# The two halves of a tile's attention scores joined in TensorE's order, in a fused two-layer kernel

## The chip, the cores and the metric

The kernel runs on one core of one Trainium2 chip, as one launch. The metric is device time in microseconds (us). Timed three times, the kernel before took 2907.69, 2910.03 and 2917.73 us; the median, 2910.03, is what a change is held against.

## The reference

The input x has 2048 rows of 128 numbers. Four blocks work on it, all in f32:

```
xn = layernorm(x);  x = x + attention0(xn) + experts0(xn)       # 16 heads, causal over 2048; 8 experts, top 2
xn = layernorm(x);  x = x + mamba(xn) + transformer(xn)

def transformer(x):                                             # 6 layers
    for i in range(6):
        x = attn_layer(shift_tokens(x), Wqkv[i], q_scale[i], k_scale[i], Wo[i]) + x
        x = ffn_layer(shift_tokens(x), ln_g[i], ln_b[i], W1[i], b1[i], W2[i], b2[i]) + x

def attn_layer(x, ...):                                         # 16 heads of 64
    q, k, v = split(x @ Wqkv)                                   # 128 -> 3 x 1024
    q, k = rotate(l2norm(q) * q_scale), rotate(l2norm(k) * k_scale)
    # windows of 32 rows: each query sees its own window and the one before it, masked to a band
    sim = einsum('bhwie,bhwje->bhwij', q, [k of the last window, k]) * 8
    return softmax(sim) @ [v of the last window, v] @ Wo
```

`ffn_layer` is a layer norm, a gated product of 128 to 2 x 341 and back to 128. The change touches only `sim`'s place in the order of work.

## The kernel before, in words

There are two stages, divided by a barrier of all engines. The first, up to about 1145 us, holds attention0, the experts and half of mamba. The second, `transformer_*`, holds the six layers with the other half of mamba woven in. The change lies in the second stage alone.

The second stage goes through 96 tiles (`NTILE`: 6 layers of 16 tiles of 128 rows) in a software pipeline. One turn of the loop `for n in range(LAST_STEP)` in `transformer_pe` is a step. The order on each engine is written out by hand: nothing is planned by costs, and no engine takes anything out of its order. Between engines there are semaphores (`E.wait_ge`, `.then_inc`). TensorE's order in step n is:

1. `scores_first(n)`: 8 bf16 matmuls write the mask into the score banks (L1372); then it waits for the turned queries and keys (semaphores `qT`, `kT`, `halo`) and `score_half` issues 32 small matmuls, of 64 rows by 32 columns, for the first eight heads (L1363). An f32 matmul stands in the profile as two MATMUL and two LDWEIGHTS records, so this half is 64 of each.
2. `project_q(n + 2)`: the queries of the tile after next, 128x128 by 128x512, four records of each kind (L1348).
3. `scores_second(n)`: the other 32 small matmuls (64 records), after which `lscore` tells VectorE that the scores are there.
4. `side(n)`: one transpose of a coming input (L1426), sometimes a product for mamba (L1434), and the output projection of the tile before (L1442, 16 records).
5. `project_k(n + 2)` (L1348), then `turn_probs(n)` (L1389), whose transposes wait for the exponentials.
6. `project("v", n + 1)` (L1348), `values(n, 0)` (L1400, 64 records), the feed-forward part (`forward`: L1456, L1457, L1463, L1448), `values(n, 1)` (L1400), the transposes of the next queries and keys (L1356), the transposes of the output (L1409).

VectorE's order in a step: mamba's scan of the unit (L476), `shift` (a maximum over the scores, L1833, and the subtraction in two halves, L1839), `finish` (the residual, L1880, behind L1442), `rotate("q", n + 2)` (L1852 to L1854, behind the queries' squares), the copies of the turned probabilities (L1873), and so on. ScalarE's order: `square("q", n + 2)` (L1630) first, behind the queries' projection; then mamba's two decays (L457), the turned input (L1638, behind L1426), and the exponentials (`probs`, L1673, behind `shift`). GpSimd adds and scales the rotated queries and keys (L2030, L2049). SyncE issues the DMAs.

PSUM is taken as four pairs of banks. `pair_table` gives each product its pair by the parity of n: the scores and `turn_probs` have one pair, the queries' projection another, `side` a third. `pair(key, *until)` waits until the last holder's contents have been read, and notes what has to be read before the pair is free again.

Of the kernel before, what the change touches and what calls it, by code (L numbers as in the profile page):

```python
# [34 lines left out]
DH = 64  # L35
INNER = H * DH
WIN = 32
# [4 lines left out]
NTILE = L * NT  # L42
# [1122 lines left out]
def halos(n):  # L1165

    return n - n // NT
# [161 lines left out]
def transformer_pe(k):  # L1329
    E, s, ps = k.te, k.sem, k.ps  # L1330
    held = {}

    def pair(key, *until):

        p = k.pair[key]
        for name, value in held.get(p, ()):
            E.wait_ge(s(name), value)
        held[p] = until
        return ps[:, 2 * p:2 * p + 2, :]

    def project(what, n, *until):
        l = n // NT
        at = ("q", "k", "v").index(what) * INNER
        to = pair((what, n), *until)
        E.wait_ge(s("xcT"), n + 1)
        E.wait_ge(s(f"wqkv{l % 2}"), 32 * (l // 2 + 1) if l else 16)
        for c in range(2):
            mm = E.matmul(to[:, c, :], k.xcT[:, n % 4, :], k.wqkv[l % 2][:, at + 512 * c:at + 512 * (c + 1)], start=True, stop=True)  # L1348
        mm.then_inc(s(what + "_mm"), 1)
# [6 lines left out]
            mm = E.transpose(to[:, j // 4, j % 4 * P:(j % 4 + 1) * P], k.ra[:, n % 2, w, j * P:(j + 1) * P], k.ident[:])  # L1356
        mm.then_inc(s(f"rows_{what}"), 1)

    def score_half(n, half, to):
        for j in range(4 * half, 4 * half + 4):  # L1360
            for w in range(4):
                for o in range(2):
                    mm = E.matmul(to[WIN * w:WIN * (w + 1), o, j * DH:(j + 1) * DH], k.qT[o * DH:(o + 1) * DH, j, WIN * w:WIN * (w + 1)],  # L1363
                                  k.kT[o * DH:(o + 1) * DH, n % 2, j, WIN * w:WIN * w + DH], start=False, stop=True, skip_group_check=True)
        return mm

    def scores_first(n):
        to = pair(("scores", n), ("shifted_s", 2 * n + 2))
        for w in range(4):
            for o in range(2):  # L1370
                here, of = slice(o * DH, (o + 1) * DH), o * DH + (WIN if w else 0)
                E.matmul(to[WIN * w:WIN * (w + 1), o, :], k.identb[here, of:of + WIN], k.band[here, 0 if n % NT == 0 else 1, :], start=True, stop=False,  # L1372
                         skip_group_check=True)
        E.wait_ge(s("qT"), n + 1)
        E.wait_ge(s("kT"), n + 1)
        if halos(n):
            E.wait_ge(s("halo"), halos(n))
        score_half(n, 0, to)

    def scores_second(n):  # L1380
        p = k.pair["scores", n]
        score_half(n, 1, ps[:, 2 * p:2 * p + 2, :]).then_inc(s("lscore"), 1)

    def turn_probs(n):
        to = pair(("turn_probs", n), ("prT", 2 * n + 2))
        for c in range(8):
            if c % 4 == 0:
                E.wait_ge(s("exp"), 2 * n + c // 4 + 1)
            mm = E.transpose(to[:, c // 4, c % 4 * P:(c % 4 + 1) * P], k.pr[:, c * P:(c + 1) * P], k.ident[:])  # L1389
            if c % 4 == 3:  # L1390
                mm.then_inc(s("prob_mm"), 1)

    def values(n, o):
        to = pair((f"values{o}", n), (f"on{o}", n + 1))
        E.wait_ge(s("prT"), 2 * n + o + 1)
        E.wait_ge(s(f"vw{n % 2}"), 160 * (n // 2 + 1))
        for c in range(4):
            for w in range(4):
                for i in range(2):
                    mm = E.matmul(to[WIN * w:WIN * (w + 1), i, c * (DH + 1):(c + 1) * (DH + 1)],  # L1400
                                  k.prT[i * DH:(i + 1) * DH, 4 * o + c, WIN * w:WIN * (w + 1)],
                                  k.vw[i * DH:(i + 1) * DH, n % 2, w, 4 * o + c, :], start=True, stop=True, skip_group_check=True)
        mm.then_inc(s(f"values{o}"), 1)

    def turn_out(n):
        to = pair(("turn_out", n), ("oT", n + 1))
        E.wait_ge(s("on1"), n + 1)
        for c in range(8):
            mm = E.transpose(to[:, c // 4, c % 4 * P:(c % 4 + 1) * P], k.on[:, c * P:(c + 1) * P], k.ident[:])  # L1409
        mm.then_inc(s("out_turned"), 1)  # L1410

    def side(n):

        until = []
        if n >= 1:
            until.append(("ys", n))
        if n + 3 < NTILE:
            until.append(("xcT", n + 4))
        if new_frame(n + 1) and n + 1 < NTILE:
            until.append(("halo", halos(n + 1)))  # L1420
        if n in CHUNK_OUT:
            until.append(("mo", CHUNK_OUT[n] - NCH // 2 + 1))
        to = pair(("side", n), *until)
        if n + 3 < NTILE:
            E.wait_ge(s(f"xc{(n + 3) % 2}"), 48 * ((n + 3) // 2 + 1))
            E.transpose(to[:, 1, 0:P], k.xc[:, (n + 3) % 2, :], k.ident[:]).then_inc(s("xc_turned"), 1)  # L1426
        if new_frame(n + 1) and n + 1 < NTILE:
            E.wait_ge(s("kT"), n + 1)
            E.matmul(to[:, 1, P:3 * P], k.turn[:], k.kT[:, n % 2, :, P:KW], start=True, stop=True, skip_group_check=True).then_inc(s("halo_mm"), 1)
        if n in CHUNK_OUT:  # L1430
            E.wait_ge(s("y_gated"), CHUNK_OUT[n] - NCH // 2 + 1)
            for t in range(2):
                for a in range(ET):
                    mm = E.matmul(to[:, 0, (1 + t) * P:(2 + t) * P], k.yg[:, a, t * P:(t + 1) * P], k.wout[:, a, :], start=a == 0, stop=a == ET - 1,  # L1434
                                  skip_group_check=True)
            mm.then_inc(s("mo_mm"), 1)
        if n >= 1:
            l = (n - 1) // NT
            E.wait_ge(s("oT"), n)
            E.wait_ge(s(f"wqkv{l % 2}"), 32 * (l // 2 + 1))  # L1440
            for c in range(8):
                mm = E.matmul(to[:, 0, 0:P], k.oT[:, c * P:(c + 1) * P], k.wo[:, l % 2, c, :], start=c == 0, stop=c == 7, skip_group_check=True)  # L1442
            mm.then_inc(s("fin_mm"), 1)
# [34 lines left out]
    def forward(n):  # L1478

        what, m = forward_step(n)  # L1480
        if n >= NTILE + 4:
            if what:
                j = int(what[2])
                up(m, j, pair(("extra", n), ("hv", 3 * m + j + 1)))
            down_last(n - NTILE - 4)
        elif n % 4 == 2:
            until = [("xfT", m + 1)] if what else []
            if m >= 1:
                until.append(("x_down", m))
            to = pair(("extra", n), *until) if until else None  # L1490
            if m >= 1:
                down(m - 1, to)
            if what:
                turn_normal(m, to)
        elif what:
            j = int(what[2])
            up(m, j, pair(("extra", n), ("hv", 3 * m + j + 1)))

    def project_q(n):
        project("q", n, ("rotated_q", n + 1))  # L1500

    def project_k(n):
        project("k", n, ("rotated_k", n + 1))
# [18 lines left out]
    def turn_hat():  # L1522
        to = pair(("extra", HAT_STEP), ("turned_out", TURNED + 4))
        E.wait_ge(s("hat"), 1)
        for q in range(2):
            for c in range(4):
                mm = E.transpose(to[:, q, c * P:(c + 1) * P], k.hat[:, 4 * q + c, :], k.ident[:])
            mm.then_inc(s("turned"), 1)
# [35 lines left out]
    turn_rows("k", 0)  # L1564
    for n in range(LAST_STEP):
        if n < NTILE:
            scores_first(n)
        if n + 2 < NTILE:
            project_q(n + 2)
        if n < NTILE:  # L1570
            scores_second(n)
        if n <= NTILE:
            side(n)
        if n + 2 < NTILE:
            project_k(n + 2)
        if n < NTILE:
            turn_probs(n)
        if n + 1 < NTILE:
            project("v", n + 1, ("v_out", n + 2))
        if n < NTILE:  # L1580
            values(n, 0)
        if n != NTILE - 1:
            forward(n)
        if n == HAT_STEP:
            turn_hat()
        if n in IN_EXTRA:
            project_in("extra", n, IN_EXTRA[n])
        if n < NTILE:
            values(n, 1)
        if n + 1 < NTILE:  # L1590
            turn_rows("q", n + 1)
            turn_rows("k", n + 1)
        if n in IN_LATE:
            E.wait_ge(s("small"), 80)
            project_in("late", n, IN_LATE[n])
        if n == FACTOR_STEP:
            factors(n)
        if n in RATE_STEPS:
            rates(n, RATE_STEPS[n])
        if n < NTILE:  # L1600
            turn_out(n)
        if n == NTILE - 1:
            forward(n)
# [742 lines left out]
```

## Time and profile before

| what | value |
|---|---|
| timed runs | 2907.69, 2910.03, 2917.73 us |
| profiled execution, first to last instruction (span) | 2911.7 us |
| TensorE busy | 2789.5 us, 96% |
| VectorE, ScalarE, GpSimd busy | 2336.3, 1746.4, 1680.3 us |
| mean granted TensorE clock | 0.996 of full |
| matmul records, weight-load records | 40886, 40886 |

The profiled execution is told by its span; of time outside it the profile shows nothing. The span is 1.7 us above the median of the timed runs. "Busy" is the time in which an engine had at least one instruction in work. The ends of matmuls are modelled, so the distance from one start to the next tells more than a duration does.

### The profile page before, as it was taken

The page shows a single profiled execution, that of the slowest core. Times are in us where ns is not written, and L with a number is a line of the kernel's source. Part 1 is how long each engine was busy: PE and PEld are TensorE (multiplying, and loading weights), DVE is VectorE, ACT ScalarE, POOL GpSimd, SP SyncE. Part 2 cuts the span into 40 slices and gives each one's busy share as a digit, 9 for nine tenths or more (in the row PEclk, how much of TensorE's full clock was granted, in tenths as well). Part 3 has the DMA queues.
Part 4 walks back from the last instruction along what each step waited for, and adds up shares of the span by engine and source line. Part 5 has one row for each costly group of instructions (what it writes and reads, how often), then busy time and mean ns, then how long its engine had stood idle before and what let it go on. Part 6 is the DMA issues. An engine that isn't in the chain of part 4 may idle for free.

```text
span 2911.7 us, 98296 instructions
## 1 busy us (share of the span) xinstructions
PE 2789.5 (96%) x40886; PEld 1832.5 (63%) x40886; DVE 2336.3 (80%) x3830; ACT 1746.4 (60%) x2618; POOL 1680.3 (58%) x1454
## 2 busy tenths in 40 slices
PE   8999999999999999899999999999999999999997
PEld 5556565655665655566656666666666666666665
DVE  6777755774677776998968999889998999898884
ACT  4455555555666665556666666666666666666663
POOL 1000002000466665676767888878887888788882
PEclk9999999999999999999999999999999999999999
DMA  3000000000011111243234434333443343333332
GB/s 97 1 1 1 1 1 3 1 1 10 21 45 46 45 46 31 77 129 79 73 103 106 99 86 114 84 93 88 114 95 91 92 118 91 88 89 83 89 85 66
DMA packets 183114, 188.24 MB, mean 65 GB/s; under 512 B 77517, under 2 KB 130515, under 8 KB 181139
## 3 DMA queue, kind: packets, MB, share of 16 engines
q1 hardware_dynamic: 182675, 181.94, 24.8%
q8 instruction: 329, 5.39, 0.8%
q14 instruction: 110, 0.90, 0.1%
HBM read 61.00 MB, written 6.03 MB: 23 GB/s over the span
## 4 chain that ended last, share of the span: by engine, by line
PE 73%; DVE 10%; issue 5%; POOL 5%; SPq 3%; ACT 3%; DMA 1%; DVEq 0%; POOLq 0%; ACTq 0%
PE ps L1348 13%; PE ps L587 13%; PE ps L1356 5%; PE ps L1400 5%; PE ps L1442 4%; PE ps L1363 4%; PE ps L622 4%; PE ps L600 4%; PE ps L1389 2%; PE ps L1456 2%; PE ps L1409 2%; PE ps L534 2%; PE ps L605 2%; PE ps L1457 2%; DVE nmx L695 2%
## 5 line engine op out<-in xcount | busy, mean ns | idle before, releaser
L1348 PE MATMUL ps<-wqkv,xcT 128*128 128x512 f32 x1152 | 553.2, 603 | 4.7 <-DVE area L1886 1.6
L587 PE MATMUL ps<-xnT,qp 128*128 128x512 f32 (+3 forms) x1280 | 527.1, 543 | 17.2 <-ACT prob L814 16.3
L2030 POOL TENSOR_TENSOR ra<-ra,rb 128x1024 f32<-128x1024 f32 x191 | 452.4, 2375 | 121.9 <-DVE rb L1854 121.0
L814 ACT ACTIVATE prob<-ps,ebias,shift 128x1024 f32<-128x1024 f32 (+7 forms) x384 | 360.3, 955 | 124.0 <-DVE ebias L704 60.4
L822 ACT ACTIVATE probT<-ps 128x512 f32<-128x512 f32 (+3 forms) x384 | 207.9, 541 | 353.6 <-PE ps L600 353.5
L587 PEld LDWEIGHTS ps<-xnT,qp 128*128 128x128 f32 x1280 | 231.7, 191 | 273.6 <-issue 228.5
L2049 POOL TENSOR_TENSOR ra<-ra,rn 128x1024 f32<-128x1024 f32 x192 | 362.3, 1908 | 8.9 <-DVE ra L1946 1.2
L695 DVE TENSOR_REDUCE nmx<-ps 128x1 f32<-128x1024 f32 (+7 forms) x256 | 245.8, 987 | 108.3 <-PE ps L587 93.3
L1348 PEld LDWEIGHTS ps<-wqkv,xcT 128*128 128x128 f32 x1152 | 196.7, 190 | 154.3 <-issue 143.5
L1630 ACT ACTIVATE sq<-ps 128x1024 f32<-128x1024 f32 x192 | 195.6, 1019 | 85.6 <-PE ps L1348 85.3
L1852 DVE TENSOR_TENSOR ra<-ps,tab 128x1024 f32<-128x1024 f32 x192 | 233.6, 1217 | 3.7 <-issue 3.1
L1400 PEld LDWEIGHTS ps<-vw,area 64*32 64x32 f32 x12288 | 137.3, 105 | 149.7 <-issue 129.1
L1861 DVE TENSOR_REDUCE ss<-sq 128x16 f32<-128x1024 f32 x192 | 224.2, 1209 | 0.0
L600 PE MATMUL ps<-ident,prob 128*128 128x128 f32 x1344 | 217.7, 279 | 5.6 <-ACT probT L822 5.6
L1363 PEld LDWEIGHTS ps<-kT,qT 64*32 64x32 f32 x12288 | 139.5, 105 | 120.0 <-issue 119.3
L600 PEld LDWEIGHTS ps<-ident,prob 128*128 128x128 f32 x1344 | 149.1, 141 | 80.9 <-issue 67.2
L713 DVE COPY probT<-ps 128x512 f32<-128x512 f32 (+3 forms) x256 | 151.1, 590 | 53.3 <-PE ps L605 49.8
L1356 PE MATMUL ps<-ident,ra 128*128 128x128 f32 x1536 | 190.0, 277 | 3.3 <-DVE rb L1854 2.5
L1647 ACT ACTIVATE vs<-ps 128x1024 f32<-128x1024 f32 x96 | 98.4, 1025 | 156.4 <-PE ps L1348 149.7
L1673 ACT ACTIVATE area<-area 128x512 f32<-128x512 f32 x192 | 117.7, 630 | 122.7 <-DVE area L1839 122.7
L1363 PE MATMUL ps<-kT,qT 64*32 64x64 f32 x12288 | 171.5, 224 | 20.0 <-issue 18.9
L622 PE MATMUL ps<-probT,vb 128*32 128x128 f32 x4352 | 190.4, 278 | 0.0
(274 smaller groups left out, 5651.9 us busy)
## 6 DMA issues: line engine op xcount, KB each, us to landing
vw<-vs SPq DMA_DIRECT2D x576, 130.0 KB
vw<-vs SPq DMA_DIRECT2D x384, 65.0 KB
bc<-bc_scratch SPq DMA_DIRECT2D x128, 128.0 KB, 2.9
area<-bc_scratch SPq DMA_DIRECT2D x128, 128.0 KB, 4.3
wqkv<-lwqkv_dram SPq DMA_DIRECT2D x6, 1536.0 KB, 8.6
xc<-xs SPq DMA_DIRECT2D x96, 32.0 KB
wo<-lwo_dram SPq DMA_DIRECT2D x6, 512.0 KB, 9.6
xc<-xs SPq DMA_DIRECT2D x96, 31.8 KB
```

The lines of the kernel that those rows point to most:

```text
L587: mm = E.matmul(ps[:, 2 * r + o // 512, 0:w], k.qp[:, group % 2, g % NTH * P:(g % NTH + 1) * P], k.xnT[:, k0 + o:k0 + o + w], start=True, ...
L600: mm = E.transpose(ps[:, 4, c * P:(c + 1) * P], k.prob[:, r, c * P:(c + 1) * P], k.ident[:])
L622: mm = E.matmul(ps[32 * c:32 * c + 32, 6 + b, 0:P], k.vb[:, group % 2, block, 0:32] if odd else k.vb[:, group % 2, block, VW:VW + 32], k.p ...
L695: V.tensor_reduce(k.nmx[:, b, mine.index(U):mine.index(U) + 1], of, X_AXIS, ALU.max, negate=True).then_inc(s("v"), k.v.up())
L814: A.activation(k.prob[:, r, 0:nk], ps[:, 2 * r:2 * r + 2, :].rearrange("p a b -> p (a b)")[:, 0:nk], ACT.Exp, bias=k.ebias[:, row % 2:row ...
L1348: mm = E.matmul(to[:, c, :], k.xcT[:, n % 4, :], k.wqkv[l % 2][:, at + 512 * c:at + 512 * (c + 1)], start=True, stop=True)
L1356: mm = E.transpose(to[:, j // 4, j % 4 * P:(j % 4 + 1) * P], k.ra[:, n % 2, w, j * P:(j + 1) * P], k.ident[:])
L1363: mm = E.matmul(to[WIN * w:WIN * (w + 1), o, j * DH:(j + 1) * DH], k.qT[o * DH:(o + 1) * DH, j, WIN * w:WIN * (w + 1)], k.kT[o * DH:(o + 1 ...
L1400: mm = E.matmul(to[WIN * w:WIN * (w + 1), i, c * (DH + 1):(c + 1) * (DH + 1)], k.prT[i * DH:(i + 1) * DH, 4 * o + c, WIN * w:WIN * (w + 1) ...
L1852: V.tensor_tensor(out_a, of, bcast(tab[:, 2 * w, :], 1, H), ALU.mult)
L2030: G.tensor_tensor(k.ra[:, n % 2, w, :], k.ra[:, n % 2, w, :], k.rb[:, w, :], ALU.add).then_inc(s("added_" + what), 1)
L2049: G.tensor_tensor(of, of, bcast(k.rn[:, n % 2, H * w:H * (w + 1)], 2, DH), ALU.mult).then_inc(s("normal_" + what), 1)
```

## The change

In `transformer_pe`, `scores_first`, `scores_second` and `score_half` become one function `scores`, in which the 64 small matmuls follow each other without a break, and the queries' projection comes behind it. The waits ahead of the first half stay where they were; the semaphore `lscore` is raised by the last small matmul, as before. No instruction is added or taken away, and no other engine's order is touched.

```diff
-    def score_half(n, half, to):
-        for j in range(4 * half, 4 * half + 4):
-            for w in range(4):
-                for o in range(2):
-                    mm = E.matmul(...)
-        return mm
-
-    def scores_first(n):
+    def scores(n):
         to = pair(("scores", n), ("shifted_s", 2 * n + 2))
...
         E.wait_ge(s("kT"), n + 1)
         if halos(n):
             E.wait_ge(s("halo"), halos(n))
-        score_half(n, 0, to)
-
-    def scores_second(n):
-        p = k.pair["scores", n]
-        score_half(n, 1, ps[:, 2 * p:2 * p + 2, :]).then_inc(s("lscore"), 1)
+        for j in range(8):
+            for w in range(4):
+                for o in range(2):
+                    mm = E.matmul(...)
+        mm.then_inc(s("lscore"), 1)
...
     for n in range(LAST_STEP):
         if n < NTILE:
-            scores_first(n)
+            scores(n)
         if n + 2 < NTILE:
             project_q(n + 2)
-        if n < NTILE:
-            scores_second(n)
         if n <= NTILE:
             side(n)
```

## Rows read from the trace of the kernel before

**Rows 1.** The page's busy us, share of the span and instructions of each engine.
```profile
PE 2789.5 (96%) x40886; PEld 1832.5 (63%) x40886; DVE 2336.3 (80%) x3830; ACT 1746.4 (60%) x2618; POOL 1680.3 (58%) x1454
```
**Rows 2.** The 96 steps' stretch: busy us (records) by engine, clock, DMA.
```profile
1180.60:2905.60 1725.00, 1660.57 (x32213) 1130.94 (x32214) 1506.96 (x2325) 1081.07 (x1520) 1356.80 (x1162) 1.00 0.37 92
```
**Rows 3.** TensorE's waits, 1180 to 2860: line, releaser, total us, times, longest.
```profile
PE ps L1363 <- issue: 16.6, 24, 1.1
PE ps L1389 <- ACT area L1673: 13.2, 15, 2.5
PE ps L1400 <- issue: 6.8, 11, 2.3
```
**Rows 4.** Timeline, TensorE, 2200 to 2240: start, duration, engine, line, count [idle before].
```profile
2200.72 0.91 PE L1363 MATMUL ps<-kT,qT 64*32 64x64 f32 x64
2201.57 1.98 PE L1348 MATMUL ps<-wqkv,xcT 128*128 128x512 f32 x4
2203.48 0.86 PE L1363 MATMUL ps<-kT,qT 64*32 64x64 f32 x64
2204.27 0.33 PE L1426 MATMUL ps<-ident,xc 128*128 128x128 f32 x1
2207.11 1.88 PE L1348 MATMUL ps<-wqkv,xcT 128*128 128x512 f32 x4
2208.41 0.14 PEld L1389 LDWEIGHTS ps<-ident,area 128*128 128x128 f32 x1 [0.24 <-issue]
2208.83 1.04 PE L1389 MATMUL ps<-ident,area 128*128 128x128 f32 x8
2227.77 1.88 PE L1348 MATMUL ps<-wqkv,xcT 128*128 128x512 f32 x4
2229.58 0.86 PE L1400 MATMUL ps<-vw,area 64*32 64x65 f32 x64
```
**Rows 5.** Timeline, TensorE, 2044.5 to 2053.5: a step with a stall.
```profile
2044.61 0.85 PE L1363 MATMUL ps<-kT,qT 64*32 64x64 f32 x64
2045.39 1.98 PE L1348 MATMUL ps<-wqkv,xcT 128*128 128x512 f32 x4
2047.31 0.45 PE L1363 MATMUL ps<-kT,qT 64*32 64x64 f32 x30
2048.86 0.51 PE L1363 MATMUL ps<-kT,qT 64*32 64x64 f32 x34 [1.11 <-issue]
```
**Rows 6.** Queue of instruction fetches: whole run, 1180.6 to 2905.6, 2045.7 to 2045.9.
```profile
q8 instruction: 329, 5.39, 0.8%
...
q8 instruction: 257, 4.21, 1.1%
...
q8 instruction: 1, 0.02, 49.2%
```
**Rows 7.** Timeline, TensorE, of the last two tiles, where no projection stands between the halves.
```profile
2849.45 1.73 PE L1363 MATMUL ps<-kT,qT 64*32 64x64 f32 x128
...
2870.43 0.35 PE L1363 MATMUL ps<-kT,qT 64*32 64x64 f32 x17 [2.25 <-issue]
```
**Rows 8.** Timeline, VectorE and ScalarE between scores and exponentials, in the step of rows 4.
```profile
2203.62 1.00 ACT L1630 ACTIVATE sq<-ps 128x1024 f32<-128x1024 f32 x1
2204.38 1.22 DVE L1833 TENSOR_REDUCE nmxl<-ps 128x16 f32<-128x1024 f32 x1 [2.55 <-PE ps L1363]
2204.53 0.90 ACT L457 ACTIVATE acc<-area,alog 128x256 f32<-128x256 f32 x2
2205.32 0.26 ACT L1638 ACTIVATE xcT<-ps 128x128 f32<-128x128 f32 x1
2206.36 1.23 ACT L1673 ACTIVATE area<-area 128x512 f32<-128x512 f32 x2 [0.78 <-DVE area L1839]
```
**Rows 9.** Timeline, 1746 to 1751: a step in which TensorE waits for the exponentials.
```profile
1746.01 0.33 PE L1426 MATMUL ps<-ident,xc 128*128 128x128 f32 x1
1747.98 1.21 DVE L1833 TENSOR_REDUCE nmxl<-ps 128x16 f32<-128x1024 f32 x1
```

More of the change, by code:

```diff
@@ L1357, in turn_rows @@
         mm.then_inc(s(f"rows_{what}"), 1)
-    def score_half(n, half, to):
-        for j in range(4 * half, 4 * half + 4):
-            for w in range(4):
-                for o in range(2):
-                    mm = E.matmul(to[WIN * w:WIN * (w + 1), o, j * DH:(j + 1) * DH], k.qT[o * DH:(o + 1) * DH, j, WIN * w:WIN * (w + 1)],
-                                  k.kT[o * DH:(o + 1) * DH, n % 2, j, WIN * w:WIN * w + DH], start=False, stop=True, skip_group_check=True)
-        return mm
-    def scores_first(n):
+    def scores(n):
         to = pair(("scores", n), ("shifted_s", 2 * n + 2))
@@ L1377, in scores_first @@
             E.wait_ge(s("halo"), halos(n))
-        score_half(n, 0, to)
-    def scores_second(n):
-        p = k.pair["scores", n]
-        score_half(n, 1, ps[:, 2 * p:2 * p + 2, :]).then_inc(s("lscore"), 1)
+        for j in range(8):
+            for w in range(4):
+                for o in range(2):
+                    mm = E.matmul(to[WIN * w:WIN * (w + 1), o, j * DH:(j + 1) * DH], k.qT[o * DH:(o + 1) * DH, j, WIN * w:WIN * (w + 1)],
+                                  k.kT[o * DH:(o + 1) * DH, n % 2, j, WIN * w:WIN * w + DH], start=False, stop=True, skip_group_check=True)
+        mm.then_inc(s("lscore"), 1)
     def turn_probs(n):
```

## The prediction

> **What bounds the kernel now.** I read the page's shares first. TensorE is busy 96% of the span [rows 1]. In the 96 steps it is busy 1660.6 of 1725.0 us at full clock, against 1507.0 for VectorE [rows 2]. So the steps go by TensorE: a shorter wait elsewhere is worth something only where TensorE waits for it, and only 64 us are idle. Next come TensorE's own waits [rows 3]. The wait that this change seems to aim at, probability transposes waiting for exponentials, is 13.2 us in 15 steps. The largest is another: 16.6 us before the score matmuls, in 24 places, released by "issue", that is by nothing the profile names. Last I read timelines, one of a clean step [rows 4] and one with such a stall [rows 5]. The stall lies inside the second half of the scores: 30 records, a hole, 34 records. It is the same instruction form without a wait of its own, so neither data nor a semaphore holds it.
>
> **What the hole is.** The fetch queue moved 329 packets and 5.39 MB, 16.4 KB each, for 81,772 matmul and weight-load records: 249 records to a packet [rows 1, 6]. In the steps it is 257 packets for 64,427 records, 251 to a packet; the remainder can be waits, so a packet is about 256 instructions. I counted TensorE's stream between the holes in the score and value matmuls: nearly all lie a whole number of such packets apart. In the step of rows 5 a packet starts in 2045.7 to 2045.9, 1.1 us behind the first score, and the matmuls go on at 2048.86, about 3.1 us after it started [rows 5, 6]. So a crossing into a new packet has to wait until roughly 3 us after that packet's transfer began. Small matmuls reach the crossing sooner than anything else here: 64 of them, with 64 loads, take 0.79 us (2203.48 to 2204.27, [rows 4]), so one packet of them lasts 1.6 us. For the crossings that lie in the second half and wait, I found the transfer starting 0.9 to 2.3 us behind the first score, in the first half or just after it. The projection between the halves, 1.91 us (2201.57 to 2203.48), is what covers most of this wait today.
>
> The Trainium skill (Runtime: NRT & Kernel Launch, section Instruction fetch mechanics) also speaks of 16 KiB blocks of 256 instructions, fetched while the last one executes, but calls the cost of a crossing "mostly hidden". The trace agrees on the size and disagrees on the cost: 16.6 us stand open at the scores alone [rows 3]. By the page's rule the joined scores would cost nothing; that is the first rival below.
>
> **The change part by part.**
>
> *One change of tile shape fewer.* Before: halves, projection, half, transpose. A projection between full-array neighbours has a pitch of 1.72 us (2207.11 to 2208.83); the next weights are loaded 0.42 us before it ends. Ahead of small matmuls it is 1.81 (2227.77 to 2229.58), and between small ones on both sides 1.91 [rows 4]. So a full product costs 0.10 when small ones precede it and 0.09 when they follow. After the change the queries' projection has the scores before it and L1426 behind: 1.82. That is 0.09 a step in 94 steps, 8.5 us. L1426 now follows a full product and may gain another 0 to 0.05 a step; I take 2 us. Together -10 us, with bounds of 8 and 14.
>
> *Crossings that lose their cover.* The steps hold 257 packets, and 128 of the about 685 instructions of a step (257 x 256 / 96) are the second half. So 257 x 128 / 685 = 48 crossings fall there, 47 in steps with a projection. The order of instructions up to the first half does not change, so the packet arrives when it did; the matmul behind the crossing is reached 1.9 us earlier. Where it stalls already, it goes on at the same moment, and the projection, which ran ahead of the stall, now runs behind it: the whole 1.9 us are lost. In the step of rows 5 the hole would begin at 2044.61 + 0.79 + 30 x 0.0123 = 2045.8 instead of 2047.7, and end at 2048.86 all the same. That is 24 x 1.9 = 45.6 us, taking the 24 waits [rows 3] as all in the second half (those that I looked at were, but for a few). For the other 23 crossings the packet was there 0 to 2.5 us early; spread evenly, the mean loss is 1.9 x 1.9 / 2 / 2.5 = 0.7, 16 us. Together +62 us. Bounds: nothing, if the fetch moves forward with the scores, and 47 x 1.9 = 89. The last two tiles show the joined form already [rows 7]: 128 records and then L1442, one at 2849.45 in 1.73 us with no hole, one with a hole of 2.25 us behind record 111. I take the middle term, which is nearest to what rows 5 and 7 show.
>
> *Scores ready earlier.* In a step without a crossing, `lscore` comes 1.9 us earlier against everything behind it. VectorE waited 2.55 us for it in the step of rows 4 [rows 8], but ScalarE's exponentials stand behind the queries' squares, the decays and the turned input. By the same step's rows: the projection ends at 2200.72 + 2 x 0.79 + 1.82 = 2204.1 [rows 4]; squares (1.00) to 2205.2, decays (0.90) to 2206.1, the input (0.26) to 2206.4 [rows 8]. The exponentials then start at 2206.4, against 2206.36 before: nothing gained where there are decays. And the wait of rows 3 is mostly not for the scores: at 1746 they are done at 1746.01 and VectorE, still at the scan, begins the maximum at 1747.98 [rows 9]. Earlier scores do not help such a step. What helps it is the delay: where TensorE loses 1.9 us, some waits for exponentials and some value stalls are absorbed. Of the 13.2 + 6.8 us [rows 3] I give back 10, bounds 0 and 20.
>
> *What else moves.* The projection ends 0.7 us later in a clean step (the second half passes it, the shape term comes off), so squares, rotation and GpSimd's add of the queries start later by that; they are used a step later, at L1356. Cover: VectorE is then still at `shift` and `finish`, which wait for L1442 as before. If that cover failed, 94 x 0.7 = 66 us would be the ceiling, but no wait of rows 3 belongs to that chain, so I take 0. No DMA is moved and no PSUM pair changes its holder's order.
>
> **Sum.** -10 + 62 - 10 = +42 us on the profiled 2911.7, 2953.7. The span stands 1.7 us over the median of the timed runs, so I forecast 2952 us, 1.4% slower.
>
> **Rivals.**
>
> *The crossings stay covered* (the time falls). If TensorE's queue reads on ahead and requests the packet earlier once the small matmuls run without a break, only the shape term and a little of the exponentials' wait remain: 2910 - 10 - 5 = 2895. For it: the fetch needs a request, and I see only its transfer. Against: the transfer starts in the first half already, which is not moved, and the hole of 2.25 us in rows 7. Chance 0.12. Faster.
>
> *Half covered.* The packet comes forward by about 1 us of the 1.9, or the absorbed waits are twice as large: the loss is 62 x 0.5 = 31, less 20, + 11: 2921. Chance 0.10; most of it is still slower by over 0.3%, a part lies within.
>
> *Every crossing loses all,* and the waits absorb nothing: 89 - 10 = +79, 2989. For it: instruction transfers share the DMA with 92 GB/s of data [rows 2], so they may come later. Chance 0.08.
>
> *The queries arrive late.* The later projection holds VectorE behind `finish`, and TensorE waits at L1356: up to +66 on top, if VectorE's 1507 of 1725 us leave no slack. This decides once VectorE's slack in a step is under 0.7 us. It is inside the range's upper part; chance 0.04.
>
> The forecast itself has 0.66, with 2930 to 2975 as its own range.
>
> **How the numbers follow.** About 0.3%, 9 us, is what a measurement of this kernel can tell from no change. Faster by more: 0.12. Within: 0.05 out of the half-covered case. Slower: 0.66 + 0.05 + 0.08 + 0.04 = 0.83. The range reaches from the half-covered case's 2918 to 2980, which leaves out the faster rival and the highest sums.
>
> **What would show it.** In the profile after: the wait of L1363 on "issue" grows from 16.6 us in 24 places to about 80 in 45, the longest near 3 us; the projection's pitch behind the scores falls from 1.91 to 1.82 in every step; the fetch queue has the same 257 packets; in steps without a crossing the step is 0.1 us shorter; the exponentials' wait shrinks. I am wrong if the issue wait stays near 17 us: then the packets come forward with the scores. I am wrong in the other way if a wait for VectorE appears at L1356 or L1442.

## The result, and the profile after

| | before | after |
|---|---|---|
| timed runs | 2912.2 us (2907.69 to 2917.73, 4) | 2975.05 us (2968.95 to 2985.89, 4) |
| profiled execution's span | 2911.7 us | 2967.2 us |
| PE busy | 2789.5 us | 2792.3 us |
| mean granted TensorE clock | 0.996 | 0.987 |

The ratio is 1.0225 (95% interval 1.019 to 1.026): 2.2% slower. The forecast was 2952 us with 2918 to 2980 as its range; the direction and the main mechanism were right, the size was short by 23 us, at the very end of the 2930 to 2975 that the main case had given itself.

The page after has the same number of instructions; TensorE does the same work and stands idle longer. The first line is the page's busy time; then the 96 steps' stretch (columns as in [rows 2]):

```profile
PE 2792.3 (94%) x40886; PEld 1851.3 (62%) x40886; DVE 2326.8 (78%) x3830; ACT 1736.3 (59%) x2618; POOL 1679.0 (57%) x1454
...
1177.90:2961.20 1783.30, 1666.05 (x32215) 1151.32 (x32208) 1497.68 (x2325) 1071.81 (x1520) 1355.42 (x1162) 0.98 0.36 89
```

The steps take 1783.3 us instead of 1725.0 [rows 2], 58 more, while TensorE's busy time grew by 5. All of the difference lies in them. TensorE's waits from 1180 to 2915 (line, releaser, total us, times, longest) say where; the score matmuls are now L1373, the projections still L1348:

```profile
PE ps L1373 <- issue: 63.0, 33, 3.0
PE ps L1382 <- ACT area L1664: 13.0, 12, 2.1
PE ps L1348 <- issue: 8.9, 6, 2.8
PE ps L1393 <- issue: 5.9, 11, 2.1
```

Against [rows 3], the wait with no named releaser grew from 16.6 to 63.0 us before the scores, and the one before the projections from 1.3 to 8.9 (a crossing among the last score instructions shows there). The wait for the exponentials (L1382) did not move: 13.2 and 13.0. The fetch queue moved the same 257 packets in the steps.

Two steps of the timeline show it (TensorE; start, duration, line, count, idle before). The first is a step without a crossing in the scores:

```profile
2049.65 1.59 PE L1373 MATMUL ps<-kT,qT 64*32 64x64 f32 x128
2051.17 1.98 PE L1348 MATMUL ps<-wqkv,xcT 128*128 128x512 f32 x4
2052.99 0.27 PE L1419 MATMUL ps<-ident,xc 128*128 128x128 f32 x1
2053.10 1.95 PE L1435 MATMUL ps<-wo,area 128*128 128x128 f32 x16
```

The projection's pitch is 2052.99 - 2051.17 = 1.82 us, as forecast, and L1419's is 0.11. The second is the tile of [rows 5], with the same crossing in it:

```profile
2067.91 1.29 PE L1373 MATMUL ps<-kT,qT 64*32 64x64 f32 x99
2071.77 0.45 PE L1373 MATMUL ps<-kT,qT 64*32 64x64 f32 x29 [2.57 <-issue]
2072.15 2.66 PE L1348 MATMUL ps<-wqkv,xcT 128*128 128x512 f32 x4
2074.61 0.42 PE L1419 MATMUL ps<-ident,xc 128*128 128x128 f32 x1
```

The hole lies at instruction 2 x 99 = 198 of the scores; in [rows 5] it was 2 x 64 + 8 + 2 x 30 = 196, the same but for the order of loads. The matmuls go on 3.9 us behind the first one, against 4.25 before: the crossing is reached 1.9 us sooner, and the packet is there only 0.4 us sooner. Before, the projection was done by then; now it still has all its time to do. Its pitch is 2.46 here, not 1.82, because the granted clock fell: it was 0.50 from 2073.3 to 2076.7. Clearer after another hole, where the windows view (stretch, length, busy us of PE, PEld, DVE, ACT, POOL, then the granted clock) stands below the timeline:

```profile
1370.16 0.68 PE L1373 MATMUL ps<-kT,qT 64*32 64x64 f32 x32 [2.61 <-issue]
1370.77 3.36 PE L1348 MATMUL ps<-wqkv,xcT 128*128 128x512 f32 x4
1373.97 0.27 PE L1419 MATMUL ps<-ident,xc 128*128 128x128 f32 x1
```
```profile
1366.60:1370.20 3.60, 0.99 (x92) 0.83 (x71) 3.40 (x7) 2.62 (x4) 0.79 (x1) 1.00 0.27 72
1370.30:1373.60 3.30, 3.30 (x36) 1.57 (x34) 2.51 (x3) 0.00 (x0) 3.05 (x5) 0.50 0.02 5
```

TensorE did 0.99 us of work in 3.6 at 2.4 GHz (the 1.00 in the row), and then ran at 1.2 GHz (0.50), for 3.4 us by the clock's record. The projection took 3.20 us (to 1373.97), 1.4 more than at full clock.

### The profile page after: what moved, and what is told of

Read it like the earlier page. It is cut to its first block, busy times and chain, and to the rows that moved or that the text cites. A ratio compares the mean times of both kernels' runs of the same rounds, so it can differ in the third digit from the quotient of the medians.

```text
span 2967.2 us, 98296 instructions
## 1 busy us (share of the span) xinstructions
PE 2792.3 (94%) x40886; PEld 1851.3 (62%) x40886; DVE 2326.8 (78%) x3830; ACT 1736.3 (59%) x2618; POOL 1679.0 (57%) x1454
## 4 chain that ended last, share of the span: by engine, by line
PE 74%; DVE 9%; issue 7%; POOL 5%; ACT 3%; SPq 2%; DMA 1%; DVEq 0%; POOLq 0%; ACTq 0%
PE ps L1348 15%; PE ps L587 13%; PE ps L1356 5%; PE ps L1435 5%; PE ps L1393 5%; PE ps L1373 4%; PE ps L622 4%; PE ps L600 4%; PE ps L1382 2%; PE ps L1449 2%; PE ps L1402 2%; PE ps L534 2%; PE ps L605 2%; PE ps L1450 2%; DVE nmx L695 2%
## 5 line engine op out<-in xcount | busy, mean ns | idle before, releaser
L1348 PE MATMUL ps<-wqkv,xcT 128*128 128x512 f32 x1152 | 572.3, 621 | 12.3 <-issue 8.9
L1348 PEld LDWEIGHTS ps<-wqkv,xcT 128*128 128x128 f32 x1152 | 201.2, 195 | 168.6 <-issue 158.4
L1373 PE MATMUL ps<-kT,qT 64*32 64x64 f32 x12288 | 161.7, 226 | 63.9 <-issue 63.0
L1435 PEld LDWEIGHTS ps<-wo,area 128*128 128x128 f32 x1536 | 185.9, 196 | 29.2 <-issue 28.2
L1373 PEld LDWEIGHTS ps<-kT,qT 64*32 64x32 f32 x12288 | 141.9, 105 | 95.1 <-issue 92.8
L1435 PE MATMUL ps<-wo,area 128*128 128x128 f32 x1536 | 192.2, 279 | 1.3 <-issue 1.3
```

## The experiments

Each was timed beside the kernel before on the same chip; the ratios are to it. The theory: TensorE's instructions come in packets of 256, a crossing into the next packet must wait until that packet has arrived, and the projection between the halves had covered this. The main rival: the projection, now later, delays the chain behind it.

### The cover taken away in part, or replaced

**three_quarters.** The projection behind 48 of the 64 small matmuls.

```diff
-        for j in range(4 * half, 4 * half + 4):
+        for j in (range(6), range(6, 8))[half]:
```

> The kernel before, with the queries' projection behind 48 of the 64 small matmuls of the scores instead of 32; the last 16 stand behind it. Packet theory (a crossing into a new instruction packet that was hidden by the projection is now reached 1.9 us too early): only the crossings that lie in the 16 moved matmuls lose, 17 of the 50 or so of the joined kernel, and by the slack that I read for each in the trace of before they lose 18 us, with the clock's share some 22: 2930 to 2940 us, a third of the joined kernel's loss; the wait of L1363 on issue grows from 16.6 to about 32 us. Rival (the later projection, which delays squares and rotation): the projection is later by 0.4 us, half of the joined kernel's delay, so half of the loss: about 2943. Rival (the number of changes of tile shape): unchanged against before, so 2912.

Measured: 2937.83 us, ratio 1.0113 (1.0077 to 1.0148). The sum over the crossings gave 2930 to 2940. Half the delay of the projection would have given 2943, which the interval does not exclude, so the time speaks against the tile shape alone (2912). The waits speak for the packets: on issue, 26.3 us before the scores and 9.1 before the projections (1180 to 2860), 17.5 more than before in the same stretch, against the 18 expected, while the wait for the exponentials did not grow (11.1 against 13.2).

**side_between** and **side_first.** `side(n)` takes the projection's place between the halves; or it stands between the joined scores and the projection.

```diff
             scores_first(n)
+        if n <= NTILE:
+            side(n)
+        if n < NTILE:
+            scores_second(n)
         if n + 2 < NTILE:
             project_q(n + 2)
-        if n < NTILE:
-            scores_second(n)
-        if n <= NTILE:
-            side(n)
```
```diff
             scores(n)
+        if n <= NTILE:
+            side(n)
         if n + 2 < NTILE:
             project_q(n + 2)
-        if n <= NTILE:
-            side(n)
```

> First half of the scores, then side(n) (L1426, L1434, L1442: 1.95 us of full-array products), second half, then the queries' projection, then the keys'. Packet theory: what hides a crossing in the second half is any long product, so 1.95 us of it do as well as the projection's 1.91: 2905 to 2920, equal to before, and L1363's wait on issue stays at 15 to 20 us. Rival (the later projection): the projection ends 2.7 us later than in the kernel before, three to four times the delay of the joined kernel: 2975 or more.

> All 64 small matmuls without a break, as in the changed kernel, but side(n) before the queries' projection. Packet theory: the scores are joined, so the same crossings are reached too early, whatever follows: as the changed kernel, 2965 to 2985. L1373's wait on issue about 60 to 65 us. Rival (the later projection costs the time): the projection is another 1.95 us later than in the changed kernel, so clearly slower than it, 3000 or more.

Measured: side_between 2997.01 us, ratio 1.0304 (1.0274 to 1.0334); side_first 3062.26 us, 1.0531 (1.0501 to 1.0562). Both expectations of my theory missed: the rival is real when the projection is late by this much. TensorE's waits of side_between, 1180 to 2860:

```profile
PE ps L1389 <- ACT area L1673: 74.3, 89, 2.2
PE ps L1426 <- ACT area L1679: 16.9, 61, 0.3
PE ps L1363 <- issue: 8.0, 24, 0.8
```

and of side_first:

```profile
PE ps L1382 <- ACT area L1664: 72.1, 87, 2.2
PE ps L1373 <- issue: 57.2, 26, 3.5
PE ps L1435 <- issue: 18.1, 12, 2.1
```

The two prices can be read apart, in the same 1680 us of each. With `side` ahead of the projection the wait for exponentials goes from 13 us to 74 with the scores split and to 72 with them joined. With the scores joined, the unnamed wait goes from 8.0 to 57.2 + 18.1. The ratios add up in the same way: joining costs 2.25% with `side` behind and 5.31 - 3.04 = 2.27% with `side` ahead; moving `side` costs 3.04% and 5.31 - 2.25 = 3.06%. Each ratio is good to some 0.3%. So joining costs the same with the projection equally late on both sides (side_first against side_between), and the 8.0 us say that `side`'s products cover a crossing at least as well as the projection did (16.6).

**exps_first.** side_between, with ScalarE's exponentials ahead of the squares.

```diff
-        if n + 2 < NTILE:
-            square("q", n + 2)
         for u in units(n + 1):
...
         if n < NTILE:
             probs(n)
         if n + 2 < NTILE:
+            square("q", n + 2)
             square("k", n + 2)
```

> side_between, and on ScalarE the exponentials ahead of the squares of the queries. If side_between lost its 89 us because the exponentials stand behind the squares, which stand behind the late projection, then the wait of L1389 for the exponentials (74.3 us in 89 places) falls to under 15 us and the time to 2905 to 2925. If the late projection costs it in another way (rotation, GpSimd's add, the transposes of L1356), the wait moves there and the time stays over 2960.

Measured: 3051.76 us, ratio 1.0494 (1.0473 to 1.0515). The wait for exponentials did go, from 74.3 to 3.2 us, but it moved. TensorE's first line, then VectorE's:

```profile
PE ps L1400 <- DVE rb L1853: 105.8, 83, 1.7
```
```profile
DVE ra L1851 <- issue: 128.8, 86, 2.5
```

VectorE now stands 129 us before the rotation. The profile names no releaser; by the kernel it waits for the squares, which now come last, and in the step looked at it starts at 2214.36, just as the queries' squares are done (begun at 2213.26, 1.0 us long). TensorE's values wait for VectorE: they need the projection's PSUM pair, which the rotation reads. So in both orders that were tried a projection 2.7 us late is paid for. One 0.7 us late, as in the changed kernel, shows in no wait of TensorE.

### The projection ahead of all small matmuls

**queries_first.**

```diff
                 E.matmul(to[...], k.identb[...], k.band[...], start=True, stop=False, skip_group_check=True)
+        if n + 2 < NTILE:
+            project_q(n + 2)
         E.wait_ge(s("qT"), n + 1)
```

> Mask, queries' projection, then all 64 small matmuls, then side(n). Packet theory: the crossings in the second half are reached as late as in the kernel before (the projection runs ahead of all small matmuls), and the request for the next packet can go out while the projection runs, so they wait less: L1363's line on issue below 10 us; one change of tile shape fewer gives 9 us: 2912 - 9 - 10 + 5 (the projection now waits for the keys' copy, which holds its PSUM pair) = 2898, range 2885 to 2912. Rival (joined scores are slow in themselves, by a conflict between small matmuls that the projection had broken up): as the changed kernel, 2965 to 2985. Rival (later projection): it is earlier here than before, so 2912 or a little less.

Measured: 2916.77 us, ratio 1.0026 (1.0012 to 1.004). Joined scores as such are not slow: with the projection ahead, the loss is 0.26% instead of 2.25%. The time lies above the expected range (2885 to 2912), for two reasons that its waits show. The scores wait 14.5 us on issue in 23 places, not under 10, and the projection's pair is held by the keys' copy for longer than I gave it:

```profile
PE ps L1348 <- ACT kT L1654: 14.7, 65, 0.8
PE ps L1375 <- issue: 14.5, 23, 1.2
```

**keys_first** turns and copies the keys ahead of the queries, to free that pair.

```diff
-            turn_rows("q", n + 1)
             turn_rows("k", n + 1)
+            turn_rows("q", n + 1)
...
-            queries_out(n + 1)
             keys_out(n + 1)
+            queries_out(n + 1)
```

> queries_first (mask, queries' projection, all small matmuls), and the rows of the keys turned and copied ahead of the queries' on TensorE and ScalarE, so that the projection finds its PSUM pair free. Packet theory: L1348's wait for the keys' copy (14.7 us in 65 places in queries_first) goes, L1375's wait on issue stays near 14: 2917 - 15 = 2902, some 0.2 to 0.4% faster than before. If the wait only moves to the queries' copy ahead of the small matmuls, it stays at 2917.

Measured: 2935.05 us, ratio 1.0079 (1.0065 to 1.0093): a miss. The wait moved to the first mask matmul, behind the copy of the queries' rows (L1364, 43.6 us in 88 places), at the scores' own PSUM pair, which the queries' rows hold longest:

```profile
PE ps L1364 <- ACT qT L1644: 43.6, 88, 1.4
```

### The packets moved, the order kept

Four kernels hold the order and move the packets. Some 42 small bf16 matmuls a step, written over by the mask, make each step a whole number of 256 instructions, so that a crossing lies at the same instruction of the scores in every step: 40 or 200 behind their start. A step is then three packets long (before, 2.7), and its other two crossings move along with this one. "Split" is the kernel before, "joined" the changed one.

```diff
+FILL = [...]   # 4059 in all for 40, 3979 for 200, so that each step's crossing falls where it should
...
         to = pair(("scores", n), ("shifted_s", 2 * n + 2))
+        for i in range(FILL[n]):
+            w, o = i // 2 % 4, i % 2
+            E.matmul(to[WIN * w:WIN * (w + 1), o, 0:DH], k.identb[...], k.band[...], start=True, stop=True, skip_group_check=True)
```

> The changed kernel, with some 42 small extra bf16 matmuls (64 rows, 64 columns) a step ahead of the mask, overwritten by it: as many as make every step a whole number of 256 instructions, so that the crossing into a new packet lies 40 instructions behind the start of the scores in every step. The matmuls themselves cost about 0.5 us a step, 50 in all. Packet theory: no crossing lies in the last 3/4 of the scores, so L1373's line waits on issue under 5 us instead of 63; 2975 + 50 - 63 - clock's share 15, with up to 20 for crossings in the values: 2945 to 2970. Rival (the joined scores or the later projection cost the time, wherever the packets lie): 3025, as the changed kernel plus 50.

> The same as joined_at_40 with 80 fewer extra matmuls in all, so that the crossing lies 200 instructions behind the start of the scores in every step. Packet theory: it is reached 1.2 us after the first score, while the packet is there at 3.4 to 4.0, so every step waits 2.2 to 2.8 us: 96 steps, 210 to 270 us in L1373's line, and more for the clock: 3170 to 3300. Rival (place of the packets does not matter): equal to joined_at_40 within 10 us.

> The kernel before with the extra matmuls of joined_at_40, crossing 40 instructions behind the start of the scores. Packet theory: no crossing in the second half, so joining the halves brings here what the change of shapes gives: this one 5 to 15 us slower than joined_at_40. Rival (later projection or joined scores as such): this one 60 us faster than joined_at_40.

> The kernel before with the extra matmuls of joined_at_200: the crossing lies in the second half of the scores in every step, 3.1 us after the first score. Packet theory: 0.3 to 1.0 us of wait in every step, 30 to 95 us in L1363's line, and faster than joined_at_200 by 94 x 1.9 = 180 us or, with the clock, more. Rival: equal to split_at_40 within 10 us.

| crossing behind the scores' start | split | joined | joined minus split |
|---|---|---|---|
| 40 instructions | 2957.05 (ratio 1.0165, 1.0129 to 1.02) | 2943.77 (1.0119, 1.006 to 1.0178) | -13 us, not clear of noise |
| 200 instructions | 2906.94 (1.0003, 0.9986 to 1.002) | 3062.43 (1.0527, 1.0494 to 1.056) | +155 us |
| as it falls (before, after) | 2912.2 | 2975.05 | +63 us |

This settles it. By nothing but where the packets begin, the same edit costs 155 us or nothing that can be told from zero. At 40 there are two runs of each kernel; the medians stand 13 us apart, single runs 4 to 23, and the two intervals overlap. The scores' waits, 1180 to 2900, in the order joined_at_200, split_at_200, joined_at_40, split_at_40:

```profile
PE ps L1378 <- issue: 140.7, 85, 2.9
PE ps L1364 <- issue: 13.7, 34, 1.5
PE ps L1378 <- issue: 42.0, 38, 1.7
PE ps L1364 <- issue: 34.7, 32, 1.7
```

A step of joined_at_200 and one of split_at_200, TensorE:

```profile
2114.14 1.37 PE L1378 MATMUL ps<-kT,qT 64*32 64x64 f32 x100
2117.06 0.45 PE L1378 MATMUL ps<-kT,qT 64*32 64x64 f32 x28 [1.55 <-issue]
2117.43 1.98 PE L1349 MATMUL ps<-wqkv,xcT 128*128 128x512 f32 x4
```
```profile
2060.08 1.98 PE L1349 MATMUL ps<-wqkv,xcT 128*128 128x512 f32 x4
2061.99 0.45 PE L1364 MATMUL ps<-kT,qT 64*32 64x64 f32 x31
2062.60 0.46 PE L1364 MATMUL ps<-kT,qT 64*32 64x64 f32 x33 [0.17 <-issue]
```

The hole lies behind 2 x 100 = 200 instructions in the first, and behind 2 x 64 + 8 + 2 x 31 = 198 in the second, where it is short: the projection ran ahead of it. In joined_at_200, 95 of 96 steps have a hole at record 100 and the scores have almost none elsewhere; in joined_at_40, 37 of the 38 holes in the scores lie behind record 19 or 20. Three sizes missed. joined_at_40 and split_at_40 still wait at the scores, where under 5 us were expected: in a third of the steps and more the packet still came late. Why was not tried; the DMAs which spread the values at that time may delay it. Their other crossings wait too: in joined_at_40, 19.9 us at the values and 10.4 at the output projection. joined_at_200 cost less than 3170, since its waits average 1.7 us, not 2.5. And split_at_200 waits 13.7 us, not 30 to 95. The extra matmuls cost less than the 0.5 us a step that I gave them (48 take 0.36 us, and the mask behind them 0.22 instead of 0.40: some 15 us net in all).

**split_at_150** uses this: the crossing is to come late enough behind a request that went out before the scores. The profile shows the transfers, not the requests, so that part stays the theory's.

> split_at_200 with the crossing 150 instructions behind the start of the scores in every step: the request for the packet then goes out before the scores begin, and the crossing is reached 2.8 us behind the first score. Packet theory: L1364's line waits on issue under 6 us (13.7 in split_at_200, 16.6 before); the next two crossings lie in the first values and ahead of the mask, where they may cost 0 to 15 us. 2907 - 10 = 2897, range 2888 to 2915: the time of before or 0.5% less, although the extra matmuls cost some 46 us.

Measured: 2892.33 us, ratio 0.9948 (0.9931 to 0.9966), the fastest of all, 0.5% under the kernel before in spite of 4000 extra matmuls. The wait of its scores is nearly gone:

```profile
PE ps L1394 <- ACT area L1678: 14.6, 19, 2.0
PE ps L1405 <- DMA vw<-vs: 3.1, 3, 1.4
...
PE ps L1364 <- issue: 1.8, 3, 0.9
```

## Why the prediction was right, and where its size was off

- *What bounds the kernel.* Right: of the 58 us, 53 are TensorE's idle time. Its busy time grew by only 5, but these are two larger terms of opposite sign, shape and clock.
- *One change of tile shape fewer: -10, bounds 8 and 14.* Right in kind, too small. The pitches are 1.82 and 0.11 instead of 1.91 and 0.16, 0.14 us in a clean step. The scores themselves, which I had left alone, take 1.53 us in one run instead of 0.78 + 0.79 in two. From the first score to the output projection a clean step takes 3.46 us instead of 3.65 (medians of 42 and 49 steps), 17 us in 94.
- *Crossings that lose their cover: +62.* Right in kind, somewhat too large. By the pages' groups, idle time on issue before the scores went from 18.9 to 63.0 us over the whole run and before the projections from 1.3 to 8.9: 52 us. The instruction numbers are the same in both traces, so it can be followed crossing by crossing. The 23 that waited before, in all tiles but the last, went from 16.1 to 47.6 us, 1.4 us each and not the 1.9 that I had given to 24 of them: the packet came a little sooner, and two of them no longer wait at all. Of those that had been covered 15 now wait, 22.6 us together, more than the 16 that I had let them lose. One of 2.2 us in the last tile is gone. "About 80 us in 45 places" was 72 in 39.
- *Scores ready earlier, -10 given back.* Wrong, this is one of the two steps that failed. The exponentials' wait stayed at 13 us and the values' fell from 6.8 to 5.9; over the whole run the two together did not change (22.5 and 22.7). That nothing is gained from earlier scores was right.
- *The clock: 0.* The other failed step: I had left it out. The holes grew to 2 and 3 us, TensorE fell idle, and the granted clock fell from 0.996 to 0.987. The clock's record has TensorE at 1.2 GHz in 5 stretches of the steps before, 17 us in all, and in 18 stretches after, 72 us. Held against the distances between the same matmuls' starts at full clock, the matmuls in these stretches took some 8 us too long before and some 30 after, 22 us more (an estimate, worked out from the two traces). Worked out so: -17 + 52 + 0 + 22 = 57, against 58 measured between the two profiled executions; -17 and +22 are the 5 us of busy time.
- *What else moves: 0.* Right at 0.7 us of delay, as no wait of TensorE for that chain grew. VectorE does wait longer for the output projection (88.0 us in 53 places, 3.9 in 6 before) and less for the scores (40.6, 78.3 before), in idle time that it has. At 2.7 us the delay costs 3.0%, some 88 us.
- *The sum.* Its nearness is partly luck. Shape and crossings were 7 and 10 us too high, the waits given back 10 too low and the clock 22 too low; the first two hide half of what the last two miss.
- The rival of the page *Runtime: NRT & Kernel Launch* of the Trainium skill (Instruction fetch mechanics), a crossing that is "mostly hidden", holds for most crossings and not for those that fall on small matmuls: after the change 39 of the 257 in the steps wait at the scores or at the projection behind them. Its packet of 256 instructions is confirmed: filling every step to a multiple of 256 put the hole at one record in every step.

The timed medians stand 63 us apart, the profiled spans 55.5: the profiled execution is the fastest of the four of after (2968.95; they spread to 2985.89), so the working above explains its distance and not all of the medians'. What makes the slower ones slower was not looked at; their mean clock is lower (0.984 and 0.985).

## What to carry to other kernels

Where a hole stands inside a run of equal instructions and the profile names no releaser, count the instructions between such holes; a common divisor points at instruction packets, not at data. A long run of the shortest instructions wants a long one in its midst, or a crossing that lies elsewhere: before joining such runs, ask what their interruption was hiding. And where holes on TensorE grow, as here at the scores from 1.1 to 3.0 us at the longest, the sum should have a term for the granted clock.

## What the runs showed of the hardware that I had not expected

- A crossing into a new packet stops TensorE for up to 3.0 us (3.5 in side_first), and where it stops is fixed to the instruction: the holes of before and after lie at the same instruction numbers, 256 or a multiple apart (loads, matmuls and semaphore instructions counted).
- Between the start of a packet's transfer and the crossing lie 3.1 us in the step of [rows 5, 6], and 2.5 to 2.8 us in the same tile after the change (start in 2069.0 to 2069.3). Over all crossings of the steps, before and after, none comes sooner than 2.2 us behind the start of its packet's transfer, and the median of those that stall for more than some 0.4 us is 2.6. What fills them was not found.
- The clock fell to 1.2 GHz for 3.4 us behind a 3.6 us stretch in which TensorE had 0.99 us of work. joined_at_200, with a hole in nearly every step, had a mean clock of 0.980, split_at_200 0.997:

```profile
core 0: 3058.4 us, clock 0.980
```
```profile
core 0: 2904.9 us, clock 0.997
```
